# Cross-attention in fp32, the hand-over from projections to attention: two groups of Q ahead of V's last tile, ScalarE's copies in a new order, the mask turned one tile later

## What is computed

```python
qh = _split_heads(q @ wq.T + bq, h)
kh = _split_heads(k @ wk.T + bk, h)
vh = _split_heads(v @ wv.T + bv, h)
scores = jnp.einsum('ntd,nsd->nts', qh, kh) / jnp.sqrt(jnp.asarray(depth, qh.dtype))
km = jnp.repeat(mask.astype(scores.dtype), h, axis=0)[:, None, :]
scores = scores + km * PAD
attn = jax.nn.softmax(scores, axis=-1)
ctx = jnp.einsum('nts,nsd->ntd', attn, vh)
out = _merge_heads(ctx, h) + q
out = (out - mu) / jnp.sqrt(var + LN_EPS) * gamma + beta
```

## Time and profile before

| | |
|---|---|
| three runs | 1089.82, 1091.9, 1092.0 us; median 1091.9 |
| profiled execution | 1091.3 us, of which the traced span is 1089.2 |
| mean granted TensorE clock | 0.994 of full |
| TensorE busy | 1064.5 us (98% of the span) |
| VectorE, GpSimd, ScalarE busy | 939.8 (86%), 773.8 (71%), 725.4 (67%) |
| TensorE in 40 slices of the span, tenths | 7999899999999999999999999999999999999995 |
| DMA | 171.32 MB, mean 157 GB/s |

### The profile page before, as it was taken

One profiled execution on the slowest core, in us unless ns is written; L12 is line 12 of the kernel. 1 busy time (PEld: TensorE's weight loads), 2 busy tenths in 40 slices (PEclk: granted clock), 3 DMA queues, 4 the chain that ended last, 5 costly groups with the idle time before them and its releaser, 6 DMA issues.

```text
span 1089.2 us, 27000 instructions
## 1 busy us (share of the span) xinstructions
PE 1064.5 (98%) x7541; PEld 978.4 (90%) x7541; DVE 939.8 (86%) x1778; ACT 725.4 (67%) x1149; POOL 773.8 (71%) x685
## 2 busy tenths in 40 slices
PE   7999899999999999999999999999999999999995
PEld 7888789999999999999999999999999999999994
DVE  5989878888888898888888888888888888888897
ACT  3331566777777777777777777777777777777674
POOL 3999723776777777777777777777777777777687
PEclk9999999999999999999999999999999999999998
DMA  7664645465565565555566566566555556556444
GB/s 231 217 214 179 189 142 138 111 165 155 147 165 153 158 166 163 135 153 143 145 167 166 146 150 160 152 167 167 139 153 145 140 163 167 154 144 166 120 112 145
DMA packets 176905, 171.32 MB, mean 157 GB/s; under 512 B 110004, under 2 KB 111556, under 8 KB 176868
## 3 DMA queue, kind: packets, MB, share of 16 engines
q1 hardware_dynamic: 167508, 145.55, 46.6%
q10 hardware_dynamic: 9360, 25.31, 10.3%
HBM read 96.76 MB, written 48.85 MB: 134 GB/s over the span
## 4 chain that ended last, share of the span: by engine, by line
PE 85%; POOL 7%; DVE 4%; issue 1%; DMA 1%; ACT 1%; SPq 1%; DVEq 0%; ACTq 0%; POOLq 0%
PE q_ps L950 33%; PE o_ps L1035 24%; PE t_ps L998 13%; PE s_ps L982 11%; PE s_ps L985 4%; POOL k_part L323 2%; POOL k_shift L319 2%; POOL v_out L335 1%; PE o_ps L965 1%; DMA keep_h<-in_mask 1%; POOL x_lo L354 0%; DVE stats L1107 0%; POOL wq_lo L350 0%; DVE row_max L1173 0%; DVE attn L1099 0%
## 5 line engine op out<-in xcount | busy, mean ns | idle before, releaser
L1035 PE MATMUL o_ps<-v_tiles,pt 128*128 128x66 f32 x2500 | 307.3, 270 | 0.5 <-DVE attn L1099 0.5
L1035 PEld LDWEIGHTS o_ps<-v_tiles,pt 128*128 128x128 f32 x2500 | 298.7, 192 | 0.9 <-issue 0.9
L1426 ACT COPY pt<-t_ps 128x512 f32<-128x512 f32 x315 | 184.0, 584 | 153.2 <-PE t_ps L998 150.2
L1173 DVE TENSOR_REDUCE row_max<-s_ps 128x8 f32<-128x616 f32 x256 | 204.6, 799 | 91.2 <-PE s_ps L985 80.3
L1302 POOL TENSOR_TENSOR x_lo<-xT_raw,x_hi 128x512 fp32r<-128x512 f32 x120 | 153.3, 1278 | 178.7 <-ACT x_hi L1399 178.0
L1389 ACT ACTIVATE probs<-probs 128x616 f32<-128x616 f32 x256 | 184.2, 720 | 82.5 <-DVE probs L1182 76.8
L950 PE MATMUL q_ps<-x_lo,wq_hi 128*128 128x512 f32 x496 | 221.2, 446 | 0.0
L1260 POOL TENSOR_TENSOR attn<-attn,v_late 128x512 f32<-128x512 f32 x124 | 159.5, 1287 | 74.4 <-DVE attn L1099 74.2
L1182 DVE TENSOR_TENSOR probs<-s_ps,row_max 128x616 f32<-128x616 f32 x256 | 204.6, 799 | 5.8
L950 PE MATMUL q_ps<-x_hi,wq_hi 128*128 128x512 f32 x496 | 195.7, 395 | 0.0
L950 PE MATMUL q_ps<-x_hi,wq_lo 128*128 128x512 f32 x496 | 195.5, 394 | 0.0
(11 more groups left out here) (188 smaller groups left out, 1700.9 us busy)
## 6 DMA issues: line engine op xcount, KB each, us to landing
xT_raw<-in_xT SPq DMA_DIRECT2D x128, 256.0 KB, 3.5
out<-y SPq DMA_DIRECT2D x126, 256.0 KB, 2.6
v_late<-in_x SPq DMA_DIRECT2D x31, 1024.0 KB, 6.3
k_scratch<-k_out SPq DMA_DIRECT2D x8, 1232.0 KB, 5.5
k_ac<-k_scratch SPq DMA_DIRECT2D x256, 38.5 KB, 5.6
q_a<-q_a ACTq DMA_DIRECT2D x63, 128.0 KB, 2.4
q_c<-q_a ACTq DMA_DIRECT2D x63, 128.0 KB, 2.5
q_b<-q_b ACTq DMA_DIRECT2D x63, 128.0 KB, 3.6
```

What stands on the lines that cost most here:

```text
L1035: mm = pe.matmul(bank_of(b, t)[:, col:col + tile_cols[i]], pt_of(b, h)[0:w, i, P * t:P * t + P], v_tiles[v_buffer(b, h)][0:w, i, 0:tile_co ...
L1173: dve.tensor_reduce(row_max[:, u, :].rearrange("p (j h) -> p j h", j=2), score_heads(t), AX.X, ALU.max).then_inc(max_ready, 1)
L1426: act.copy(pt[h][0:w, i, :], t_ps[0:w, :]).then_inc(pt_ready, 1)
```

## The change

Four edits, all in phase one.

1. Q's groups 0 and 1 are computed ahead of V's remaining tile, not behind it. The banks follow: `first_group(g)` numbers them 48 and 49, so they go to banks 0 and 1 in place of 4 and 5. Groups 2 and 3 stay in banks 6 and 7.
2. ScalarE copies Q0 ahead of its last four copies of K, Q1 (with the three moves behind it) ahead of the last three, two parts of x for batch 1 ahead of the last two, and the other two ahead of the last. Before, Q0, Q1 and the moves stood ahead of the last copy of K, and x behind it.
3. VectorE takes the low parts of Q0 and Q1 behind the low part of the first of these four groups of K, and its two low parts of x ahead of the last one.
4. `turn_keep` stands behind V's tile 1 of chunk 0, not behind tile 0.

```diff
--- before.py
+++ after.py
@@ -200,9 +200,13 @@
                 elif n >= 8:
                     pe.wait_ge(v_biased, c * VT + r - 2 * NG + 1)
 
+            def first_group(g):
+
+                return CHUNKS * GROUPS + g - (VT - LATE if g < 2 else 0)
+
             def first_q(g):
 
-                return bank(CHUNKS * GROUPS + g)
+                return bank(first_group(g))
 
             def keep_of(m):
                 return keep[:, m, :, :].rearrange("p i s -> p (i s)").unsqueeze(1).broadcast_to([P, HB // 2, 2 * S])
@@ -372,10 +376,18 @@
                     at_least(act, k_stored[half], DMA * c)
                     for m in range(NG):
                         n = (2 * c + half) * NG + m
-                        if n == 2 * NG * CHUNKS - 1:
+                        behind_end = 2 * NG * CHUNKS - n
+                        if behind_end == 4:
                             first_high(0)
+                        if behind_end == 3:
                             first_high(1)
                             move_first_half()
+                        if behind_end == 2:
+                            second_x(0)
+                            second_x(1)
+                        if behind_end == 1:
+                            second_x(2)
+                            second_x(3)
                         act.wait_ge(k_ready, n + 1)
                         if n == 1:
                             act.wait_ge(keep_turned, 1)
@@ -395,6 +407,13 @@
                                    ).then_inc(q_hi_ready, 1)
                     act.activation(q_b[P // 2:P, g, :], first_q(g)[P // 2:P, :], ACT.Identity,
                                    bias=bq_col[P // 2:P, g:g + 1]).then_inc(q_hi_ready, 1)
+
+                def second_x(k):
+
+                    if k == 0:
+                        act.wait_ge(k_done, 2 * NG * CHUNKS)
+                    act.wait_ge(xT_loaded[k], 2 * DMA)
+                    act.copy(x_hi1[:, k, :], xT_raw[:, k, :]).then_inc(x_hi_ready, 1)
 
                 def move_first_half():
                     act.wait_ge(q_hi_ready, 4)
@@ -426,10 +445,6 @@
                             act.wait_ge(xT_loaded[k], DMA)
                             act.copy(x_hi0[:, k, :], xT_raw[:, k, :]).then_inc(x_hi_ready, 1)
 
-                act.wait_ge(k_done, 2 * NG * CHUNKS)
-                for k in range(KC):
-                    act.wait_ge(xT_loaded[k], 2 * DMA)
-                    act.copy(x_hi1[:, k, :], xT_raw[:, k, :]).then_inc(x_hi_ready, 1)
                 first_high(2)
 
             def first_stage_of_vector(dve):
@@ -511,21 +526,29 @@
                 def values(c):
 
                     at_least(dve, v_stored, DMA * VT * c)
-                    for j in range(VT if c < CHUNKS - 1 else LATE):
+                    if c == CHUNKS - 1:
+                        last_values(c)
+                        return
+                    for j in range(VT):
                         bias_values(c, j)
                         if j < NG:
                             low_keys_out(2 * c * NG + NG + j)
-                    if c < CHUNKS - 1:
-                        return
-                    for j in range(LATE, NG):
-                        if j == NG - 1:
-                            for g in range(2):
-                                first_low(g)
-                        low_keys_out(2 * c * NG + NG + j)
+
+                def last_values(c):
+
+                    first = 2 * c * NG + NG
+                    bias_values(c, 0)
+                    low_keys_out(first)
+                    first_low(0)
+                    first_low(1)
+                    low_keys_out(first + 1)
+                    low_keys_out(first + 2)
                     for k in range(2):
                         dve.wait_ge(x_hi_ready, KC + k + 1)
                         dve.tensor_tensor(x_lo1[:, k, :], xT_raw[:, k, :], x_hi1[:, k, :], ALU.subtract
                                           ).then_inc(x_lo_ready, 1)
+                    low_keys_out(first + 3)
+
                 def first_chunk():
 
                     for j in range(NG):
@@ -619,7 +642,7 @@
                     pe.wait_ge(wq_lo_ready, 1)
                     pe.wait_ge(x_hi_ready, KC)
                     pe.wait_ge(x_lo_ready, KC)
-                    wait_for_bank(pe, CHUNKS * GROUPS + g)
+                    wait_for_bank(pe, first_group(g))
                     for k in range(KC):
                         for n, (a, b) in enumerate(terms):
                             mm = pe.matmul(first_q(g)[:, :], (wq_hi, wq_lo)[a][:, k, P * g:P * g + P],
@@ -642,6 +665,9 @@
                             for k in range(KC):
                                 key_products(c, half, m, k)
                     ctx_part = (ctx_hi[c % 2], ctx_lo[c % 2])
+                    if c == CHUNKS - 1:
+                        for g in range(2):
+                            first_queries(g)
                     for j in range(VT if c < CHUNKS - 1 else LATE):
                         if (c, j) == (0, 3):
                             pe.wait_ge(keep_v_ready, VT)
@@ -656,10 +682,10 @@
                                                (wv_hi, wv_lo)[b][:, k, :], start=(k == 0 and n == 0),
                                                stop=(k == KC - 1 and n == 2))
                         mm.then_inc(v_done, 1)
-                        if (c, j) == (0, 0):
+                        if (c, j) == (0, 1):
                             turn_keep()
 
-                for g in range(NG):
+                for g in range(2, NG):
                     first_queries(g)
```

## The result

The changed kernel takes 1093.0 us (median, 1092.5 to 1095.8) beside 1091.2 for the kernel before (1088.5 to 1092.0), 20 runs each on one chip. The ratio of the runs is 1.0025, 95% interval 1.0019 to 1.0031, which is 2.1 to 3.4 us slower. The two medians alone are 1.8 apart, the means 2.4. The time is inside the range given, but the forecast was no change, and the sign was that of rival 4. The profiled execution has a span of 1090.4 (1089.2 before).

The account below looks back on a forecast made before the run. TensorE's arrival at tile 3 of the late values was taken to bound: 5.7 us gained, 0.2 to 0.4 left behind the store. Forecast 0.3 off 1091.3 (1091.0), or 1091.6 by median; given 1091.3, range 1087.6 to 1093.6.

Parts of the forecast that it names:

- rival 4: Last store of K: x's load behind and Q's moves ahead slow its landing; at 8.6, 3.0 us slower, 1094.3; 12%.
- Mask and Q's first groups: TensorE: mask's turn at about 27.4 without the 1.27 wait; Q's third group from 113.8.
- The moves of the first half: Q's first three DMAs: issued by 116.2, landed by 118.2, so first scores start at 119.5 without a wait.
- the 5.7 us at the hand-over: TensorE between the phases: first scores 4.2 us early, with 1.5 of clock 5.7.
- the 2.5 us of waiting forecast in front of Q's half for batch 1: TensorE: arrives at 123.6, waits for VectorE's first_low(2), goes on at 126.3; about 2.5 us.
- VectorE's hold: VectorE held by GpSimd's x_lo from 119.1 to 122.1, 3.0 us; last store of K at 124.8, not 122.86.
- The landing: Last store of K: lands in 5.4 us as in the earlier trace, at 130.2.
- What stands behind the landing: GpSimd's clears and ones, then VectorE's v_late, up to TensorE's tile 3: 7.95 us after the store lands.

Follow-up runs that it names:

- e4: The kernel before with only the mask turned one tile later, behind V's tile 1; ratio to before 0.9995.
- e3: The changed kernel with the store of K's first half held until Q's first moves have landed; ratio to before 1.0010.
- f2: The changed kernel with the edits of f1 and e3 together; 1088.3 us, ratio to before 0.9977.
- f1: The changed kernel with v_late laid over K's first-half buffer and its ones set behind the first half's stores alone; 1089.8 us, ratio to before 0.9998.
- e1: The changed kernel with x's next load held until the last store of K has landed; 1091.6 us, ratio to before 1.0006.
- g1: The changed kernel with the edits of f4 and e3 together; 1091.7 us, ratio to before 1.0013.
- g2: g1 with v_late moved as in f1; 1088.6 us, ratio to before 0.9983.
- g4: The changed kernel with both holds, those of e1 and e3; ratio to before 1.0004.
- e2: The changed kernel with GpSimd's ones of v_late set ahead of its clears of v_tiles; 1091.8 us, ratio to before 1.0011.
- f4: The changed kernel with VectorE's low part of K31 ahead of its two x_lo; 1089.5 us, ratio to before 0.9995.
- g3: The kernel before with six more clears of v_tiles[0] ahead of the ones of v_late; 1093.1 us, ratio to before 1.0022.
- f3: The kernel before with v_late and its ones moved as in f1; ratio to before 1.0001.

## Why the prediction was wrong, by its own steps

**Mask and Q's first groups: right.** No wait at the turn (27.54), Q's third group at 113.66 (113.8). e4 shows that the turn alone is worth nothing that can be measured.

**The moves of the first half: mis-sized.** The step "land by 115.9 + 2.34 = 118.2" took the landing of the earlier trace rows into a place where a store of 1.2 MB had just started. Measured 6.3, so the first scores came at 122.19 and not 119.5, still with a DMA wait, and the clock fell to 0.50 there as before. Of the 5.7 us at the hand-over 1.5 were left. e3 shows the cause: with the store held, the moves land in 2.3 each and the wait is gone. It didn't decide the time, because tile 3 is bound elsewhere; f2 against f1 shows what it costs (2.3) where tile 3 isn't. Because the scores came late, the 2.5 us of waiting forecast in front of Q's half for batch 1 didn't appear either; in e3 they did, as 1.88.

**VectorE's hold: right in kind, too large.** Its two x_lo took 3.43 beside GpSimd's, 1.29 in the earlier trace rows; held 2.1, not 3.0. GpSimd's own two took 3.16, not 2.5 (half of the earlier trace rows), so the engines took turns: from 119.63 on the two have 2.5 + 1.3 + 0.5 = 4.3 to do, and need 4.1. The Trainium skill, SBUF — State Buffer, section "SBUF: two separate sides", has such instructions exclude each other; this sum agrees to 0.2. So does the stretch before it: with GpSimd's multiply through at 119.27, VectorE's two low parts (0.88) would by that rule end at 120.15, and they ended at 119.99. The store went out at 123.76 in place of the predicted 124.8, a term 1.0 too dear.

**The landing: the step that failed.** "Taken at 5.4, because that is this same store" is the term that was mis-sized: 7.8 measured. It is the same store in the program, but not in what goes with it. The text had the mechanism as rival 4, x's load close behind and the moves of Q's second half close ahead, with 12%, and had argued against it that the store "shared the queues before as well". That was true of 0.6 us only, the rest of the third move (121.14 + 2.34 = 123.48): in the kernel before nothing was issued on either queue from 1.7 us ahead of the store to 3.7 behind the earlier trace rows. e1 and e3 took the two neighbours away one by one, g1 and g2 show the same landing with and without its reader.

**What stands behind the landing: right.** Landing + 7.9 holds within 0.05 in the changed kernel, e1, e3, g1 and g4. The sum with the measured terms is 123.76 + 7.8 + 7.95 = 139.5, exactly tile 3: 1.16 later than before.

**The size.** 1.16 is less than the 2.1 to 3.4 of the runs. It isn't lost behind tile 3: from the tile that follows it to the end of the span it is 946.9 to 947.7 us in all 14 profiled executions, 946.95 before and 946.93 after. So what differs is where these tiles fall from one execution to the next, and the two profiled ones aren't typical. The one after, 1090.4, is as short as any of the 20 spans of the changed kernel (1090.4 to 1093.8, median 1091.05). The one before, 1089.2, is above the middle of 33 spans of its kernel, taken beside e1 to e4 (1086.7 to 1090.4, median 1088.6), where the shorter ones have a higher mean clock; and e4 shows an execution in which the clock didn't fall behind the first scores. Between these two medians lie 2.4 us, although they come from different rounds. A kernel whose tile 3 waits for a store can't use such luck with the clock: e1's spans lie between 1087.8 and 1089.8. That this makes the missing 1 to 2 us is argued, not shown; what makes most executions of the changed kernel longer than the profiled one is open. It also means that e1, e2, e3 and g1, with tile 3 at 137.95 to 138.35, aren't faster than the kernel before with its 138.34: their ratios are 1.0006 to 1.0013. Rival 4's own arithmetic, with the store at 123.76, would have called a landing of 7.8 no measurable change (1.2); the runs made 2.7 of it. So the mechanism of rival 4 is shown, and its price only in part.

## What to carry to other kernels

A transfer's time to landing depends on its neighbours, and not on the transfer alone. When a change moves issues, list for each DMA on the critical chain what is issued close to it on either side, before and after (here within some 2 us), and price it by a row with such neighbours. An edit that makes two engines ready earlier also makes their transfers collide; f4 and f2 got 3.3 and 5.2 us back (ratios 0.9995 and 0.9977 against 1.0025), not by doing less, but by taking the store's issue or its reader out of the crowd. And look at what memory a late buffer is laid over: v_late waited for a store only because it lay on that store's source.

## What the runs showed of the hardware

- The last store, 1.2 MB, landed in 5.4 us with nothing issued within 1.7 us (four executions), and in 7.8 to 8.2 (five) with three moves of 128 KB beside and a load of 1 MB within 1.3 us behind it, although the moves are on another queue and the load comes later in its own. Issued 1.8 us behind or more, they cost it nothing (f4, one execution).
- Neighbours aren't all: the store of K's first half, with nothing issued from 9 us ahead of it to 4.6 behind, landed in 6.2 (before), 5.9 (e4), 6.1 (g3) and 4.8 (f3), four kernels with the same order there. No run shows why.
- Small moves suffer more: 128 KB took 2.3 alone and 6.1 to 6.3 beside the store; the first of the three took 3.0.
- The issue itself gets longer beside other transfers: the third move's 0.61 in e3 and 1.49 in the changed kernel, four parts of x 1.92 before and 4.92 after, 1.77 in e1. The engine that issues stands still for it: ScalarE's next copy starts at 117.19, behind 115.66 + 1.49.
- Waits of one length on TensorE don't always end in the same clock. Behind 1.88 us the granted clock stayed at 1.00 in e3 and was 0.52 (126 to 128 us) in f2; behind 2.7 it was 0.50 (124 to 126) in the changed kernel and e1, and 1.00 in f1 and f4.
